# W_down as a seven-product block form over sliding windows of five tile pairs, with its operand sums formed in the gate/up steps

## What is computed

```
gate = x @ W_gate.T + 0.5 * (x @ A_gate.T) @ B_gate.T
up   = x @ W_up.T   + 0.5 * (x @ A_up.T)   @ B_up.T
act  = silu(gate) * up
x    = x + act @ W_down.T + 0.5 * (act @ A_down.T) @ B_down.T
```

## Time and profile before

| | |
|---|---|
| timed runs | 1717.09, 1717.53, 1723.28 us |
| the profiled execution | 1715.87 us, of which the span of its instructions is 1714.2 us |
| PE busy | 1628.6 us, 95% |
| DVE, ACT busy | 920.5 us (54%), 566.1 us (33%) |
| mean granted TensorE clock | 0.986 of full speed |
| DMA | 278.40 MB, mean 162 GB/s |
| convolution and first gate/up preparation | about 0 to 295 us |
| gate/up steps | to about 1182 us, with a break at 670 to 740 us between the two u |
| down | about 1182 to 1711 us |

### The profile page before, as it was taken

How to read it: one execution, slowest core, us unless ns; L and a number is a source line. 1 busy time by engine, 2 the same in 40 slices (tenths; PEclk the granted TensorE clock), 3 DMA queues, 4 the chain that set the end, 5 groups by cost and what they waited for, 6 DMA issues and landing times.

```text
span 1714.2 us, 21064 instructions
## 1 busy us (share of the span) xinstructions
PE 1628.6 (95%) x8224; PEld 1394.1 (81%) x8224; DVE 920.5 (54%) x1182; ACT 566.1 (33%) x678; POOL 114.4 (7%) x185
## 2 busy tenths in 40 slices
PE   2989989999999997899999999998999999999999
PEld 2988878888888886778888888886888888888887
DVE  6544686665566664876665666666325325325322
ACT  2211353333333332543333333334224224224211
POOL 5100022442120000000000000000000000000000
PEclk9999989999999998999999999999999999999999
DMA  8989654664453335233333333328448547547542
GB/s 309 366 327 334 222 188 145 194 201 157 148 166 98 99 99 187 90 93 99 98 99 98 99 99 99 99 74 273 133 134 248 148 140 241 163 133 227 174 139 60
DMA packets 156869, 278.40 MB, mean 162 GB/s; under 512 B 55554, under 2 KB 72770, under 8 KB 156226
## 3 DMA queue, kind: packets, MB, share of 16 engines
q1 hardware_dynamic: 104034, 234.19, 42.5%
q0 software_dynamic: 12672, 25.82, 4.8%
q10 hardware_dynamic: 40064, 17.04, 3.5%
HBM read 237.26 MB, written 65.31 MB: 177 GB/s over the span
## 4 chain that ended last, share of the span: by engine, by line
PE 87%; DMA 5%; DVE 4%; issue 2%; ACT 1%; SPq 0%; DVEq 0%; ACTq 0%
PE ps L806 81%; PE ps L791 6%; DMA tt<-k_pad 2%; DMA k_pad<-ksb 1%; DMA raw<-a_gu_sel 1%; DVE xlo L1523 1%; ACT whi L1001 1%; DMA xraw<-x_keep 1%; DVE wlo L1523 1%; DVE xraw L1523 1%; DMA draw<-act_keep 0%; DVE xres L1717 0%; ACT lohi L1001 0%; ACT cc L1001 0%; DMA leni<-len 0%
## 5 line engine op out<-in xcount | busy, mean ns | idle before, releaser
L806 PE MATMUL ps<-xhi,whi 128*128 128x512 f32 (+1 forms) x1080 | 421.2, 390 | 29.7 <-ACT cc L1001 10.5
L806 PE MATMUL ps<-xlo,whi 128*128 128x512 f32 (+1 forms) x1080 | 419.9, 389 | 0.0
L806 PE MATMUL ps<-xhi,wlo 128*128 128x512 f32 (+1 forms) x1080 | 418.7, 388 | 0.0
L1001 ACT ACTIVATE whi<-raw 128x1024 fp32r<-128x1024 f32 (+3 forms) x202 | 198.1, 981 | 580.8 <-PE ps L806 546.7
L1523 DVE TENSOR_TENSOR wlo<-raw,whi 128x1024 fp32r<-128x1024 f32 (+1 forms) x190 | 219.4, 1155 | 307.0 <-ACT whi L1001 306.7
L806 PE MATMUL ps<-dhi,whi 128*128 128x512 f32 (+2 forms) x760 | 288.0, 379 | 3.7 <-DVE xres L1717 3.7
L806 PE MATMUL ps<-dlo,whi 128*128 128x512 f32 (+2 forms) x760 | 286.6, 377 | 0.0
L806 PE MATMUL ps<-dhi,wlo 128*128 128x512 f32 (+2 forms) x760 | 286.4, 377 | 0.0
L806 PEld LDWEIGHTS ps<-xhi,whi 128*128 128x128 f32 x1080 | 206.7, 191 | 69.6 <-DVE gq L1645 10.1
L806 PEld LDWEIGHTS ps<-xhi,wlo 128*128 128x128 f32 x1080 | 206.1, 191 | 41.5
L806 PEld LDWEIGHTS ps<-xlo,whi 128*128 128x128 f32 x1080 | 206.6, 191 | 37.4
(11 more groups left out here) (174 smaller groups left out, 1663.8 us busy)
## 6 DMA issues: line engine op xcount, KB each, us to landing
raw<-wgu SPq DMA_DIRECT2D x84, 512.0 KB, 6.7
tt<-k_pad SPq DMA_DIRECT2D x64, 512.0 KB, 8.6
raw<-wd SPq DMA_DIRECT2D x64, 512.0 KB, 3.8
loraw<-bgu_sel SPq DMA_DIRECT2D x84, 256.0 KB, 4.5
act_keep<-up SPq DMA_DIRECT2D x42, 512.0 KB, 3.1
draw<-act_keep SPq DMA_DIRECT2D x84, 256.0 KB, 6.9
raw<-wd SPq DMA_DIRECT2D x32, 320.0 KB, 3.0
xr<-xr SPq DMA_DIRECT2D x4, 2048.0 KB, 10.5
```

The costliest lines, as they stand in the source:

```text
L806: return nc.tensor.matmul(out, w, x, start=start, stop=stop, skip_group_check=True)
L1001: return nc.scalar.activation(out, in_, ACT.Copy)
```

## The change

Down is now computed for two slabs at once, with the same seven products. The 2x2 blocks are: two output tiles (2·hp and 2·hp+1, hp = 0..3), two inner tiles (the pair i, tiles 2i and 2i+1; ten pairs cover tiles 0 to 19), two slabs (A, B). A step of down takes one hp and five of the ten pairs. So each product is five tiles deep: 15 matmuls of 512 columns. There are 16 steps (`DSTEPS`): two u, two halves of the pairs, four hp. Which five pairs a step uses is in `WINDOW`: the window slides, so that the two halves of each hp together cover all ten, and only the pairs in `NEW` are loaded for a step, seven operand tiles for each pair (three activations as they are and four sums). That is 91 tiles of 256 KB for each u, 182 in all, where 88 were loaded before.

Steps with s % 8 below 4 write their four output tiles to `y_first` in DRAM; the later four read them back as their residual, and add tile 20 and the rest of 64 rows with the adapter (`tails`). A_down runs beside steps 1 and 4 of each u (`down_a`, `down_a_tail`); since only sums of the operands are at hand for one of its blocks, it takes 216 matmuls of 256 columns for each u.

Everything that is loaded for down goes through a ring of six units (`RING`), and ACT and DVE work three units ahead of PE (`AHEAD`). A unit is the weights of one product, an A_down piece, or half a tail. Unit i+6 is loaded when PE has finished unit i.

The four sums of activations are formed on DVE after each odd gate/up step (`act_sums`) and stored to `act_sums`; `up` has two buffers for that. The four sums of W_down are formed on DVE in each of 40 gate/up steps (`weight_sums`, four operations of 128x128), loaded and stored by SP (`sums_in`, `sums_out`), 256 KB each way. In the gate/up loop of DVE, `sums_13(n+1)` and `mul(n-1)` now come ahead of `w_lo("u3", n)`.

```
+DSTEPS = 16
+PERM = [2 * i + kh for kh in range(2) for i in range(10)] + [FT - 1, FT]
+WINDOW = ((0, 1, 2, 3, 4), (0, 1, 2, 3, 4), (2, 3, 4, 5, 6), (3, 4, 5, 6, 7),
+          (5, 6, 7, 8, 9), (5, 6, 7, 8, 9), (7, 8, 9, 0, 1), (8, 9, 0, 1, 2))
+NEW = (WINDOW[0], (), (5, 6), (7,), (8, 9), (), (0, 1), (2,))
...
+def order_of_down():
+    units = []
+    for s in range(DSTEPS):
+        td = {}
+        if s % 8 == 1:
+            td = {"P1": ("A", 0), "P2": ("A", 1), "P5": ("B", 0), "P7": ("B", 1)}
+        if s % 8 == 4:
+            td = {"P5": ("A", 0), "P7": ("A", 1), "P6": ("B", 0), "P4": ("B", 1)}
+        for p in PRODUCTS:
+            units.append(("m", s, p))
+            if p in td:
+                units += [("td", s, *td[p], g) for g in range(2)]
+            if s % 8 == 4 and p == "P2":
+                units += [("tdt", s, x) for x in "AB"]
+        if s % 8 >= 4:
...
+RING = 6
+AHEAD = 3
...
+            key = ("m", s - 1, PRODUCTS[q + 4]) if q < 3 else ("m", s, PRODUCTS[q - 3])
+            at[key] += [(s, q, i) for i in NEW[s % 8]]
...
+                             up[f % 2][:, :].rearrange("p (j t) -> p j t", j=2)).then_inc(s_ast[f % 2], 16)
+                if f % 2:
+                    blk = f // 2
+                    sp.wait_ge(s_tq, 4 * (10 * u + blk) + 2)
+                    sp.dma_start(tq_d[u, blk, 0:2].rearrange("k p t -> p k t"),
+                                 gq[:, 0:2 * T].rearrange("p (k t) -> p k t", k=2)).then_inc(s_tst, 16)
+                    sp.wait_ge(s_tq, 4 * (10 * u + blk + 1))
+                    sp.dma_start(tq_d[u, blk, 2], gq[:, 2 * T:3 * T]).then_inc(s_tst2, 16)
+                    sp.dma_start(tq_d[u, blk, 3], vv[:, :]).then_inc(s_tst2, 16)
...
+                for h in range(2):
+                    src = wd_d[2 * hp + h].rearrange("p (k n) -> p k n", n=P)[:, blk:blk + 11:10, :]
+                    sp.dma_start(sw[:, 2 * h:2 * h + 2, :], src).then_inc(s_swld, 16)
...
+                if i >= RING:
+                    sp.wait_ge(s_dn, i - RING + 1)
                 else:
...
+                    sp.wait_ge(s_p, prod(N - 1, ("P2", "P7", "P7", "P4", "P3", "P3")[i]))
...
+            load_first(0, 1)
+            wait_lo("u2", N - 1)
+            sp.wait_ge(s_s24, 2 * N)
+            load_first(2, 3, 4)
+            wait_lo("lora", N - 1)
+            load_first(5)
+            sp.wait_ge(s_swst, 16 * 40)
+            load_first(6)
+            for k, p in enumerate(PRODUCTS):
+                sp.wait_ge(s_p, prod(N - 1, p))
+                load_first(*range(7 + 4 * k, 11 + 4 * k))
+                for i in {"P2": (0,), "P7": (1, 2), "P4": (3,), "P3": (4, 5)}.get(p, ()):
+                    load_unit(i)
...
+                if step + 1 < DSTEPS:
+                    for q, p in enumerate(PRODUCTS):
+                        if NEW[(step + 1) % 8] and last_use(step, p) == i:
+                            sp.wait_ge(s_dn, i + 1)
+                            for blk in NEW[(step + 1) % 8]:
+                                load_act(step + 1, q, blk)
...
+            def down_product(step, p):
+                q, window = PRODUCTS.index(p), WINDOW[step % 8]
+                slot = unit_ready(("m", step, p))
+                if NEW[step % 8]:
+                    pe.wait_ge(s_alo, ATILE[step, q, NEW[step % 8][-1]])
+                if p == "P1":
+                    if step:
+                        pe.wait_ge(s_yv, step)
+                    else:
+                        pe.wait_ge(s_v, N)
+                if p in ("P2", "P7") and step == 0:
+                    pe.wait_ge(s_c2, N)
+                if p == "P2" and step:
+                    pe.wait_ge(s_yd, step)
+                if p == "P5":
+                    if step:
+                        pe.wait_ge(s_r, result(step - 1, "b"))
+                    else:
+                        pe.wait_ge(s_c12, N)
+                if p == "P7" and step:
+                    pe.wait_ge(s_r, result(step - 1, "d"))
+                if p == "P6":
+                    pe.wait_ge(s_y1, step + 1)
+                if p == "P4":
+                    pe.wait_ge(s_yd, step + 1)
+                for k in range(5):
+                    last = passes(bank[p], cols(rhi[slot], k), cols(rlo[slot], k), ahi[place_of(q, window[k])][:, :],
+                                  alo[place_of(q, window[k])][:, :],
+                                  k == 0 and p in ("P1", "P2", "P5", "P7"))
+                signal(last)
...
+            def y_store(step):
+                u, hp = step // 8, step % 4
+                act.wait_ge(s_r, last_result(step))
+                dst = y0_d if step % 8 < 4 else out_d
+                for k, (h, x) in enumerate(RES):
+                    act.dma_start(dst[:, 2 * u + GRP[x], 2 * hp + h, :], res[:, k, :]).then_inc(s_out, 16)
...
+                for t in ACTS0[:4]:
+                    act_hi(*t)
+                unit_hi(0)
                 c1(N - 1)
-                for t in range(4, 8):
-                    d_hi(0, t)
-                dw_hi(0, ("c", 0, 1))
+                for t in ACTS0[4:12]:
+                    act_hi(*t)
+                unit_hi(1)
...
+            res_in(0)
+            for i, key in enumerate(DOWN):
+                step = key[1]
+                if key[0] == "m":
+                    p = key[2]
+                    if p == "P2" and step:
+                        y_store(step - 1)
+                    if p == "P5" and step:
+                        res_in(step)
+                    if p == "P7":
+                        y_c1(step)
+                    if p == "P4":
+                        y_v(step)
+                if i + AHEAD < len(DOWN):
+                    unit_hi(i + AHEAD)
...
+            def act_sums(n):
+                even, odd = up
+                base = 4 * (10 * (n // FT) + n % FT // 2)
+                dve.wait_ge(s_mul, n + 1)
+                dve.wait_ge(s_c12, n + 1)
+                sub(gq[:, 0:T], even[:, T:2 * T], even[:, 0:T]).then_inc(s_tq, 1)
+                sub(gq[:, T:2 * T], odd[:, T:2 * T], even[:, T:2 * T]).then_inc(s_tq, 1)
+                dve.wait_ge(s_tq, base + 1)
+                sub(gq[:, 2 * T:3 * T], odd[:, T:2 * T], gq[:, 0:T]).then_inc(s_tq, 1)
+                dve.wait_ge(s_tq, base + 3)
+                sub(vv[:, :], odd[:, 0:T], gq[:, 2 * T:3 * T]).then_inc(s_tq, 1)
...
+            def weight_sums(n):
+                i = piece(n)
+                a11, a12, a21, a22 = (sw[:, k, :] for k in range(4))
+                dve.wait_ge(s_swld, 32 * (i + 1))
+                V.tensor_tensor(a22, a21, a22, ALU.add).then_inc(s_sw, 1)
+                dve.wait_ge(s_sw, 4 * i + 1)
+                sub(a21, a11, a21).then_inc(s_sw, 1)
+                dve.wait_ge(s_sw, 4 * i + 2)
+                sub(a11, a22, a11).then_inc(s_sw, 1)
+                dve.wait_ge(s_sw, 4 * i + 3)
+                sub(a12, a12, a11).then_inc(s_sw, 1)
...
+                    if p == "P1" and step:
+                        y_last(step - 1)
+                    if p == "P6":
+                        y_d(step)
+                        y_sums(step)
+                    if p == "P3":
+                        y_v(step)
+                        if step % 8 < 4:
+                            y_bank(step, "d")
+                if i + AHEAD < len(DOWN):
+                    unit_lo(i + AHEAD)
+                if key[0] == "m":
+                    for t in ACTS_AT[key]:
+                        if t[0] == "tail":
+                            tail_lo(*t[1:])
+                        else:
+                            act_lo(*t)
```

More of the change, by code:

```diff
@@ L134, in raw_slot @@
         return 2 * (i % FT % 2)
[L135 to L152, removed]
+    return 2 * (i % FT % 2) + 1
 def raw_loads():
@@ new lines, with order_of_acts, place_of, act_loads @@
+ACTS0, ACTS_AT = acts_by_unit()
+def order_of_acts():
+    at = {key: i + 1 for i, key in enumerate(ACTS0)}
+    for unit in DOWN:
+        for key in ACTS_AT.get(unit, ()):
+            at[key] = len(at) + 1
+    return at
+ATILE = order_of_acts()
+def place_of(q, i):
+    return 5 * q + i % 5
+def act_loads():
+    count, at = [0] * 35, {}
+    for s in range(DSTEPS):
+        for q in range(7):
+            for i in NEW[s % 8]:
+                count[place_of(q, i)] += 1
+                at[s, q, i] = 16 * count[place_of(q, i)]
+    return at
@@ new lines, with last_use, result, last_result @@
+ALOAD = act_loads()
+def last_use(s, p):
+    return max(DAT[k] for k in DOWN if k[1] == s and (k[0] == "m" and k[2] == p or k[0] == "td" and p in TD_QUADS[k[2], k[3]]))
+def result(s, op):
+    n = 0
+    for r in range(s + 1):
+        ops = ("sums", "v", "d", "b") + (("e", "f") if r % 8 >= 4 else ())
+        if r == s:
+            return n + ops.index(op) + 1
+        n += len(ops)
+def last_result(s):
+    return result(s, "f" if s % 8 >= 4 else "b")
+def piece(n):
+    return n if n < FT - 1 else n - 1
@@ L623, in second @@
                 wait_lo("u3", FT - 1)
```

(31 more changed lines are left out.)

768 lines of the change are left out of this document (396 added, 372 removed).

## The result

The changed kernel takes 1738.4 us (median of four, 1736.4 to 1738.8), the kernel before 1717.3: the ratio is 1.0111, 95% interval 1.0099 to 1.0123. It is slower by about 21 us, where 18 us less were forecast. The profiled execution has a span of 1736.7 us, 22.5 more than before.

A forecast was written before the change was run, and what follows sets the result against it. PE, busy 95% of the span, was taken as the bound. 1715.9 - 44.8 - 3.7 + 4 + 5 + 2.5 + 6 + 3 + 3.5 + 6 = 1697.4 us, so 1699 in timed runs; 8-in-10 range 1680 to 1724.

The forecast's parts named there:

- The count of matmuls: Down: fewer matmuls shorten PE's list from 521.1 to 476.3 us, taking off 44.8 us.
- The steady gate/up steps: All 42 gate/up steps: the added sums fit beside PE and cost 0, with up to 20 us as bound.
- The seams: Three seams: with the loaded steps, they were to give back some 30 us in waits.
- Between the u: Between the two u of gate/up: x is loaded later behind stores of sums, 4 us, bounds 0 and 8.
- Entry: Entry of down: weights land late behind 15 tiles, so P6 of step 41 starts 5 us worse, bounds -5 and +10.
- Step 0: First step of down: ACT and DVE must split 15 more tiles and come out late, 2.5 us.
- The end: After the last matmul: four adds and four stores follow instead of one each, +3.5 us.
- `y_d` of step 8: Down, at the change of u: DVE reaches this after 34.8 us, PE asks after 32.7; called 3 us late.
- Residuals and the DMA load: Down: residual loads take 10 to 16 us in six steps, costing PE 1 us each, 6 in all, between 0 and 60.
- The change of u: Down, steps 7 to 8: all 35 tiles are new and DVE, ACT and DMA fall behind, 6 us, between 2 and 20.
- (c): Rival for down: residual loads hold DVE, costing 60 us in place of 6, so slower, 1753 us; chance 0.14.
- The estimate of 32 us for four loads: Down: by packet-by-packet turns between queues, four residual loads take some 32 us while SP's queue is never empty.

The follow-up runs named there:

- e11: Changed kernel with 2-KB residual runs from copies, down's stores and residual loads on POOL's queue, new entry order, and `y_sums` moved from P6 to P3: 1696.7 us.
- e9: Changed kernel without the sums of activations and weights in gate/up; down reads other data of the same size: 1727.4 us.
- e6: Changed kernel with x copied for 2-KB residual runs, and down's stores and residual loads issued by POOL's queue instead of ACT's: 1712.4 us.
- e4: Kernel before, with eight waits of PE put in down behind chains of small DRAM copies on POOL's queue: 1804.2 us.
- e5: Changed kernel with x written a second time by output tile during gate/up, so down's residuals are read in 2-KB runs: 1718.9 us.
- e1: Changed kernel with down's stores and residual loads issued by POOL's queue instead of ACT's, still with 256-B runs: 1730.6 us.
- e2: Changed kernel with the x residuals of down replaced by other data of the same size in 2-KB runs; output lacks x: 1719.2 us.

## Why the prediction was wrong

**The count of matmuls was right.** With it and what e11 leaves of waits, down takes 507.0 us against 529.2. **The steady gate/up steps** cost 0 as said; steps 0 to 20 cost 0.5 (1.3 by e9).

**The seams were near.** Between the u 2.2 us for 4; by e9 the sums are 4.6 there, and 2.4 that I had not priced come back, so the nearness is in part luck. Entry 6.0 for 5; the forecast had the later stores of the sums and the 15 tiles ahead of the weights in one chain, and by e9 4.8 us go with the sums. Step 0 3.9 us for 2.5, all behind `alo`. The end 4.4 for 3.5. Two readings were off without weight: `y_d` of step 8 comes 2.1 us late by the terms given (34.8 less 32.7), not 3, and 368 GB/s is not the most that the trace of before shows, which has 387 in 1170 to 1174 us.

**What failed is the step "Residuals and the DMA load": "that is 1 us of PE's time each, 6 us in all".** The forecast followed the load only to its landing, and to DVE, which needs it. The queue that issues it is the list of ACT, which also copies PSUM for PE. Two items there made it late: the wait for the stores to land (8 us after the first was issued in step 2, of which ACT stood 4), and an issue that itself takes 3.2 to 7.2 us with 256-B runs. `y_c1` came 6 to 9 us late in steps 2, 8 and 10. In the six steps that the 6 us were for, PE waited 17.3 us (6.5, 2.4, 6.4 and 1.9 in steps 2, 3, 10 and 11), and the lower clock behind these waits took 7.7 more: 25 us. The change of u, forecast at 6 us, had a wait of 8.6 us behind the same list and one of 2.1 us that every run keeps; in e6, without these items on ACT, it has three of about 2.2, near the forecast. PE's waits in down sum to 38 us where I had 17.5.

**The missing term was the clock.** The sum took each wait at its length. The matmuls behind six waits in down lost 12.7 us; e4 gives 1.5 to 2.7 us behind each wait of 6 us or more. The earlier trace rows held such a wait, 7.8 us, and the matmuls behind it, 427 ns apart at first, already lost 1.6 us in the trace of before. I had not looked at them.

Together, against the forecast 498.2 us for down (529.2 - 44.8 - 3.7 + 17.5): 20 us of waits, 13 of clock, and 4 in other distances between matmuls, which I did not take apart, give the measured 535.3. Half of the miss (39 us from 1699 to 1738) hangs on the runs of 256 B: e5 alone brings the time back by 19.5 us.

**The rivals.** (c) had the right sign, and the right source, the residual loads with short runs on ACT's queue, but the wrong victim: DVE's own wait for them shows only where ACT no longer issues them, up to 11.6 us in e1 and 34.5 us in all in e6. Its price of 60 us was too high; the same steps cost 25. The rule of the Trainium skill beside it, "DMA: Bandwidth & Descriptors", "Queues, rings and completion order", was misread: there a packet is some 9 to 17 descriptors, and I had taken every run of 256 B for one. The estimate of 32 us for four loads stands against 10.9 us in e1 (1300.71 to 1311.58, at a DMA share of 1.0 to 1.1). The same page, "Specifications", gives 512 B as the least transfer for line rate; e2 and e5 agree with its direction, with 19 us between 256-B and 2-KB runs, and no length between was run.

## What to carry to other kernels

For each DMA that is added to a compute engine's list, price three things: the wait ahead of it, its issue while the queues are busy, and everything behind it on that list that another engine waits for. Loads with short runs belong on an idle queue, or the data is laid out once where the DMA engines have air; then place the consumer where the load has landed, as late as its own reader allows. And each wait of TensorE of some 6 us or more cost about 2 us beyond its length here, and some of 2 to 4 us did so too, so a few middle-sized waits weigh more than their sum.

## What was not expected of the hardware

- Four residual loads of 256 KB held ACT's list for 3.2 to 7.2 us at their issue with 256-B runs, for 1.8 us with 2-KB runs (e5). On POOL's queue the same four took 3.5 and 2.1 us (e1, e6).
- The 32 copies of the same short runs from DRAM to DRAM, 8.4 MB in all, beside steps 24 to 39 cost no time (397.7 us), at a DMA share that was 0.47 without them.
- Stores issued by POOL at the end come out 2.3 us later than by ACT (10.2 against 7.9 us from the last matmul to the end of the span).
